# A cross-attention kernel with a small attention head section behind it: layer norms by a diagonal product, projections chunk by chunk, and the heads' exponents and copies dealt out anew

## What is computed

```python
def xattn(enc, dec):                       # enc = ctx (12544 rows), dec = layernorm(x) (128 rows)
    a = softmax(enc @ dec.T, axis=-1)      # over the 128 tokens
    return a.T @ enc
def attn(x):                               # 16 heads of 16 channels, causal
    q, k, v = split(x @ w_attn + b_attn)
    att = softmax(mask(q @ k.T / 4))
    return (att @ v) @ w_proj + b_proj
def ffn(x):
    return x @ W.T + b + (x @ V_r) @ C.T
x = x + xattn(ctx, layernorm(x))
x = x + attn(layernorm(x))
x = x + ffn(layernorm(x))
```

## Time and profile of the kernel before

| what | value |
|---|---|
| median of three executions | 108.64 us (108.2 to 108.72) |
| the profiled execution | 108.57 us |
| its span, first to last instruction | 106.6 us |
| TensorE, matmul busy | 102.2 us (96% of the span) |
| VectorE busy | 76.2 us (72%) |
| ScalarE busy | 72.7 us (68%) |
| GpSimd busy | 62.7 us (59%) |
| context and weights moved | 27.73 MB, no transfer in the last third but the result |

### The profile page before, as it was taken

How to read it: one execution, slowest core, us unless ns; L and a number is a source line. 1 busy time by engine, 2 the same in 40 slices (tenths; PEclk the granted TensorE clock), 3 DMA queues, 4 the chain that set the end, 5 groups by cost and what they waited for, 6 DMA issues and landing times.

```text
span 106.6 us, 2284 instructions
## 1 busy us (share of the span) xinstructions
PE 102.2 (96%) x756; PEld 88.2 (83%) x756; DVE 76.2 (72%) x217; ACT 72.7 (68%) x267; POOL 62.7 (59%) x45
## 2 busy tenths in 40 slices
PE   6999999999999999999999999999999999999990
PEld 1379999999999999999999999999998848756660
DVE  0413999968997777987777887777889765598331
ACT  4019999779997779777779777778879218297210
POOL 7405999949999767886767886767885020000020
PEclk9999999999999999999999999999999999999999
DMA  3999999999999999999999999950000000000001
GB/s 77 320 414 418 407 412 409 403 412 407 407 404 404 410 406 414 410 406 414 403 404 414 407 406 406 369 181 0 0 0 0 6 0 0 0 0 6 0 0 49
DMA packets 8604, 27.73 MB, mean 260 GB/s; under 512 B 1105, under 2 KB 1682, under 8 KB 8594
## 3 DMA queue, kind: packets, MB, share of 16 engines
q1 hardware_dynamic: 8594, 27.60, 66.2%
HBM read 27.46 MB, written 0.13 MB: 259 GB/s over the span
## 4 chain that ended last, share of the span: by engine, by line
PE 78%; issue 16%; DVE 2%; POOLq 1%; POOL 1%; DVEq 0%
PE bank L308 42%; PE bank L320 20%; PE bank L323 10%; PE bank L339 3%; PE bank L329 1%; PE bank L343 1%; PE bank L332 1%; PE bank L295 1%; POOLq L58 1%; POOL rstd L274 1%; DVE x L729 0%; DVE bn L581 0%; DVE x L659 0%; DVE mean_var L582 0%; DVE warm L597 0%
## 5 line engine op out<-in xcount | busy, mean ns | idle before, releaser
L282 POOL TENSOR_TENSOR rows_split<-rows_ring,rows_split 128x1024 fp32r<-128x1024 f32 (+1 forms) x25 | 58.4, 2336 | 18.3 <-ACT rows_split L490 18.3
L308 PE MATMUL bank<-query_t,cols_ring 128*128 128x128 f32 x392 | 47.7, 275 | 0.0
L308 PEld LDWEIGHTS bank<-query_t,cols_ring 128*128 128x128 f32 x392 | 45.8, 192 | 1.8 <-DVE query_t L595 0.6
L501 ACT ACTIVATE bank<-bank,neg_max 128x128 f32<-128x128 f32 x98 | 33.1, 337 | 11.1 <-DVE neg_max L619 10.9
L320 PE MATMUL bank<-rows_split,probs 128*128 128x512 f32 x92 | 34.8, 413 | 0.0
L490 ACT CAST rows_split<-rows_ring 128x1024 fp32r<-128x1024 f32 (+1 forms) x25 | 25.9, 1035 | 4.1 <-DMA rows_ring<-ctx_rows_dram 3.4
L636 DVE SCALAR_TENSOR_TENSOR probs<-bank,inv_sums,probs 128x128 fp32r<-128x128 f32 x98 | 27.6, 344 | 0.9
L323 PE MATMUL bank<-rows_split,probs 128*128 128x256 f32 x92 | 25.6, 279 | 0.0
L619 DVE TENSOR_REDUCE neg_max<-bank 128x4 f32<-128x512 f32 (+1 forms) x25 | 16.9, 675 | 12.0 <-PE bank L308 11.9
L320 PEld LDWEIGHTS bank<-rows_split,probs 128*128 128x128 f32 x92 | 17.4, 189 | 3.0
L501 ACT ACTIVATION_READ_ACCUMULATOR bank<-bank,neg_max 128x1 f32 x98 | 19.8, 202 | 0.0
(11 more groups left out here) (94 smaller groups left out, 66.1 us busy)
## 6 DMA issues: line engine op xcount, KB each, us to landing
cols_ring<-ctx_cols_dram SPq DMA_DIRECT2D x24, 512.0 KB, 14.7
rows_ring<-ctx_rows_dram SPq DMA_DIRECT2D x24, 512.0 KB, 15.2
wqk_sb<-w_qk_dram SPq DMA_DIRECT2D x1, 512.0 KB
cols_ring<-ctx_cols_dram SPq DMA_DIRECT2D x1, 256.0 KB, 10.8
rows_ring<-ctx_rows_dram SPq DMA_DIRECT2D x1, 256.0 KB, 10.3
wv_sb<-w_v_dram SPq DMA_DIRECT2D x1, 256.0 KB
wproj_sb<-w_proj_dram SPq DMA_DIRECT2D x1, 256.0 KB
wffn_sb<-w_ffn_dram SPq DMA_DIRECT2D x1, 256.0 KB
```

What stands on the lines that cost most here:

```text
L282: pool.tensor_tensor(rows_split[:, b, 0:n, 1, :], rows_ring[:, slot * STEP:slot * STEP + n, :], rows_split[:, b, 0:n, 0, :].bitcast(F32), ...
L308: last = pe.matmul(into[:, t * P:(t + 1) * P], cols_ring[:, slot * STEP + t, c, :], query_t[:, c, :], start=(c == 0), stop=(c == DC - 1))
L501: last = act.activation(on[:, t * P:(t + 1) * P], on[:, t * P:(t + 1) * P], ACT.Exp, bias=neg_max[:, b, t:t + 1], accum_out=sums[:, b, t:t ...
```

## The change

`layer_norm` no longer forms `normed`. VectorE subtracts the mean over all 256 channels into `centred`, before it waits for GpSimd, and then scales the identity with the inverse deviation into `rstd_diag`. `turn_normed` multiplies `centred` with that diagonal, a full fp32 product, where there was a transposition. The first score product and the first k product wait for the copy of the first half alone.

The projections run k chunk 0, q chunk 0, k chunk 1, q chunk 1, and each round of head scores waits for its own chunk. The bias of v comes as a 128-partition tile, added by VectorE, so the `ones` product goes.

In the heads, ScalarE takes all 16 exponents head by head; `shifted` and the reduction of `head_exp` go. VectorE copies all four groups out of PSUM. Banks, the order of the products on TensorE and that of VectorE's queue are new.

```diff
-        WARM_START, WARM_X, WARM_QUERY, WARM_EXPS, WARM_TURNS = 4, 3, 1, 5, (2, 3)
+        WARM_START, WARM_X, WARM_QUERY, WARM_EXPS, WARM_TURNS = 4, 3, 1, 5, (2, 2)
...
+                pe.wait_ge(centred_ready, n + 1)
+                pe.wait_ge(rstd_diag_ready, n + 1)
                 for c in range(DC):
-                    pe.wait_ge(normed_ready, DC * n + c + 1)
-                    pe.transpose(turn[c][:, 0:P], normed[:, c * P:(c + 1) * P], ident[:]).then_inc(turned, 1)
+                    pe.matmul(turn[c][:, 0:P], centred[:, c * P:(c + 1) * P], rstd_diag[:],
+                              start=True, stop=True).then_inc(turned, 1)
...
-            for n in [*range(DC, 2 * DC), *range(DC)]:
-                if n == DC + 1:
+            for n in [DC, 0, DC + 1, 1]:
+                if n == 1:
+
                     pe.wait_ge(wffn_ready, 1)
                 ps = q_ps[n][:, 0:P] if n < DC else k_ps[n - DC][:, 0:P]
                 for c in range(DC):
+                    if n == DC and c == 1:
+                        pe.wait_ge(turn_copied, 2)
...
-            pe.wait_ge(k_copied, 1)
-            pe.matmul(v_ps[:, 0:D], ones[:], bv_sb[:], start=True, stop=False, skip_group_check=True)
-            pe.wait_ge(k_copied, DC)
-            pe.wait_ge(q_copied, DC)
-
             for m in range(HM):
+
+                pe.wait_ge(k_copied, m // 2 + 1)
+                pe.wait_ge(q_copied, m // 2 + 1)
...
             turn_exps(1)
-            keep_warm(WARM_TURNS[1], exp_t_ps[2][:])
+            pe.matmul(x2_ps[:, 0:D], ident[:], x1_bias[:], start=True, stop=False, skip_group_check=True)
+            pe.wait_ge(x1_bias_centred_ready, 1)
+            pe.wait_ge(v_copied, 2)
+            for c in range(DC):
+                pe.matmul(x2_t_ps[c][:, 0:P], x1_bias_centred[:, c * P:(c + 1) * P], ident[:], start=True, stop=False,
+                          skip_group_check=True)
             turn_exps(2)
...
+            weigh_values(0)
+            keep_warm(WARM_TURNS[1], exp_t_ps[3][:])
             turn_exps(3)
             weigh_values(1)
+            spread_inverse(0)
+            weigh_values(2)
             spread_inverse(1)
...
-            exps_by_head(0)
-            exps_shifted(1)
-            exps_by_head(2)
-            exps_by_head(3)
-            copy_exp_t(2)
-            copy_exp_t(3)
+            for j in range(GROUPS):
+                exps_by_head(j)
...
+                dve.tensor_scalar(centred[:], src, mean_var[:, 0:1], None, ALU.subtract).then_inc(centred_ready, 1)
                 dve.wait_ge(rstd_ready, n + 1)
-                for c in range(DC):
-                    half = slice(c * P, (c + 1) * P)
-                    dve.tensor_scalar(normed[:, half], src[:, half], mean_var[:, 0:1], rstd[:, 0:1],
-                                      ALU.subtract, ALU.mult).then_inc(normed_ready, 1)
+                dve.tensor_scalar(rstd_diag[:], ident[:], rstd[:, 0:1], None, ALU.mult).then_inc(rstd_diag_ready, 1)
...
             for e in range(2):
-                dve.tensor_copy(v_pad[:, :, e, :, e * HD:(e + 1) * HD], v_view[:, :, e]).then_inc(v_copied, 1)
+                dve.tensor_tensor(v_pad[:, :, e, :, e * HD:(e + 1) * HD], v_view[:, :, e], bv_view[:, :, e],
+                                  ALU.add).then_inc(v_copied, 1)
+            copy_exp_t(0)
             dve.wait_ge(head_exp_ready, 2)
-            link(dve.tensor_reduce(head_sums[:, 0, 1, :], head_exp[:, 1], AX_X, ALU.add))
-            copy_exp_t(0)
             invert_sums(0)
             copy_exp_t(1)
+            copy_exp_t(2)
+            copy_inverse(0)
+            finish_y(0)
             dve.wait_ge(head_exp_ready, 4)
             invert_sums(1)
-            copy_inverse(0)
-            finish_y(0)
+            copy_exp_t(3)
             copy_inverse(1)
             finish_y(1)
```

More of the change, by code:

```diff
@@ L73, in perceiver_kernel @@
         x3 = sb("x3", [P, D])
-        normed = sb("normed", [P, D])
+        centred = sb("centred", [P, D])
+        rstd_diag = sb("rstd_diag", [P, P])
         normed_t = sb("normed_t", [P, DC, P])
@@ L92, in perceiver_kernel @@
         warm = sb("warm", [P, P], BF16)
-        ones = sb("ones", [1, P])
         in_head = sb("in_head", [P, P // HD])
@@ L110, in perceiver_kernel @@
         head_max = sb("head_max", [P, GROUPS, HM])
-        shifted = sb("shifted", [P, HM, P])
         head_exp = sb("head_exp", [P, GROUPS, HM, P])
@@ L134, in perceiver_kernel @@
         low_rank_ps = bank[7]
[L135 to L139 removed]
+        k_ps, q_ps, v_ps = [bank[2], bank[6]], [bank[5], bank[7]], bank[2]
+        exp_t_ps = [bank[5], bank[6], bank[7], bank[5]]
+        inv_ps = [bank[6], bank[7]]
+        y_t_ps = [bank[3], bank[4]]
+        x2_ps, x2_t_ps, ffn_ps = bank[0], [bank[1], bank[2]], bank[6]
         x_landed = sem("x_landed")
@@ L154, in perceiver_kernel @@
         rstd_ready = sem("rstd_ready")
-        normed_ready = sem("normed_ready")
+        centred_ready = sem("centred_ready")
+        rstd_diag_ready = sem("rstd_diag_ready")
         turned = sem("turned")
@@ L199, in perceiver_kernel @@
         out_stored = sem("out_stored")
-        weights = [(wqk_sb, w_qk), (bqk_sb, b_qk), (wv_sb, w_v), (bv_sb, b_v),
+        weights = [(wqk_sb, w_qk), (bqk_sb, b_qk), (wv_sb, w_v), (bv_sb, b_v.to_broadcast([P, D])),
                    (wproj_sb, w_proj), (bproj_sb, b_proj.to_broadcast([P, D])), (wffn_sb, w_ffn), (bffn_sb, b_ffn.to_broadcast([P, D])),
                    (vr_sb, v_r), (ct_sb, c_t)]
-        NCONSTS = 6
-        WARM_START, WARM_X, WARM_QUERY, WARM_EXPS, WARM_TURNS = 4, 3, 1, 5, (2, 3)
+        NCONSTS = 5
+        WARM_START, WARM_X, WARM_QUERY, WARM_EXPS, WARM_TURNS = 4, 3, 1, 5, (2, 2)
         block = ctx.enter_context(nc.Block())
@@ L254, in _ @@
             pool.memset(minus_half[:], -0.5).then_inc(consts_ready, 1)
-            pool.memset(ones[:], 1.0).then_inc(consts_ready, 1)
             pool.wait_ge(pool_step, 4)
@@ L307, in score @@
                     for c in range(DC):
+                        if s == 0 and t == 0 and c == 1:
+                            pe.wait_ge(turn_copied, 1)
                         last = pe.matmul(into[:, t * P:(t + 1) * P], cols_ring[:, slot * STEP + t, c, :],
@@ L548, in exps_by_head @@
                 last.then_inc(head_exp_ready, 1)
-            def exps_shifted(j):
-                act.wait_ge(shifted_ready, 1)
-                act.activation(head_exp[:, j], shifted[:], ACT.Exp).then_inc(head_exp_ready, 1)
-            def copy_exp_t(j):
-                act.wait_ge(exp_turned, j + 1)
-                act.copy(head_exp_t[:, j].rearrange("p m q -> p (m q)"), exp_t_ps[j][:])\
-                   .then_inc(exp_t_copied[j], 1)
-            exps_by_head(0)
-            exps_shifted(1)
-            exps_by_head(2)
-            exps_by_head(3)
-            copy_exp_t(2)
-            copy_exp_t(3)
+            for j in range(GROUPS):
+                exps_by_head(j)
             for c in range(DC):
@@ L601, in _ @@
             dve.wait_ge(eps_ready, 2)
+            dve.wait_ge(consts_ready, NCONSTS)
             dve.wait_ge(x_landed, 16)
@@ L700, in _ @@
             maximum_of_heads(1)
-            dve.wait_ge(head_max_ready, 2)
-            dve.tensor_tensor(shifted[:], by_head(head_scores[1]),
-                              head_max[:, 1, :].unsqueeze(2).to_broadcast([P, HM, P]),
-                              ALU.add).then_inc(shifted_ready, 1)
             maximum_of_heads(2)
```

25 lines of the change are left out of this document (4 added, 21 removed).

## The result

| what | before | after |
|---|---|---|
| median (20 executions each) | 108.50 us (108.07 to 109.04) | 108.90 us (108.61 to 109.53) |
| the profiled execution, its span | 108.57, 106.6 us | 108.83, 107.1 us |
| ratio after to before | | 1.0047, 95% interval 1.0033 to 1.0061 |

By the ratio the changed kernel is slower by 0.51 us (0.36 to 0.66); by the two medians it is 0.40. Both are under the 0.54 us that were set as the least that a measurement tells, but the interval is clear of 1.

A forecast was written before the change was run, and what follows sets the result against it. Bounds behind an unchanged stream: one line from norm to scores, then ScalarE, then TensorE. Terms 0 - 0.54 + 0.84 + 0.21 = +0.51 gave 109.15 us against a median of 108.64; range 108.7 to 109.9.

The forecast's parts named there:

- What bounds the kernel: Stream unchanged; behind it one line from second norm to head scores, then ScalarE to 97.34, then TensorE's back-to-back products.
- Start, 0: Start of the kernel: norm products cost 0.1 to 0.25 us, hidden; term 0, bounds 0 and +0.1.
- the cover by the fourth step's load: In the stream, TensorE waits 0.20 us at 11.82 for a transfer; a later start would shorten that wait.
- Norm to first maximum, -0.54: Second norm to first head maximum: -0.09 up to the first k product and -0.45 from the rounds.
- The rounds and chunks: Head scores: rounds 0 and 1 run in the wait for q chunk 1; -0.45 us, bounds 0 and -0.45.
- waiting for half: Second norm: k chunk 0 starts after ScalarE's copy, at 87.94 where it was 88.03 behind VectorE's copy.
- rival C: `centred` beside GpSimd's power delays it at the second norm: +0.4 us, 109.55; chance 0.13.
- Exponents, +0.84: Heads on ScalarE: group 1 by heads takes 1.38 us where at once took 0.54, without gaps; +0.84.
- VectorE's queue, +0.21: Last exponent to group 3's values: group 3's copy queues behind inverse copy 0; 3.21 us for 3.00, bounds -0.1 and +0.4.
- The end, 0: Behind group 3's values: the same TensorE products, not y, end last; term 0.
- Rival A: Behind the last exponent, TensorE's own order decides: 2.15 us instead of 3.00, -0.55 in all, 108.1; chance 0.08.
- Rival B: TensorE's clock falls to 1.2 GHz behind 101 us after a queue gap: about +2, 111; chance 0.07.

The follow-up runs named there:

- E7: E1 with TensorE taking group 1's values and the first spread ahead of group 3's transposition, replacing two products of zeros; 107.53 us, ratio to before 0.9912.
- E12: Changed kernel with group 3's copy first on VectorE and group 1's exponents at once, diagonal norm kept, a repeat run; 107.18 us, ratio to before 0.9875.
- E5: Changed kernel with the norm and transposition of before, the rest kept; 108.62 us, ratio to before 1.0008.
- E2: Changed kernel with group 1's exponents as before: `shifted`, taken at once, summed by VectorE; 108.38 us, ratio to before 0.9974.
- E1: Changed kernel with the inverse of the second sums and group 3's copy ahead of inverse copy 0 and y half 0's finish on VectorE; 108.02 us, ratio 0.9934.
- E8: The kernel of E12 without the two products of zeros ahead of group 3's transposition; 107.41 us, ratio to before 0.9884.
- E10: The kernel of E12 with the norm and transposition of before and without the two products of zeros; 106.84 us, ratio to before 0.9844.
- E11: The kernel of E12 with the norm of before and E7's TensorE order, no zeros; 107.35 us, ratio to before 0.9904.
- E4: Changed kernel with `centred` behind VectorE's wait for GpSimd, so it doesn't overlap the power; 109.42 us, ratio to before 1.0069.

## Why the prediction came out right

- *What bounds the kernel.* Right: stream unmoved, then one line, then ScalarE, then TensorE, which waits for VectorE's queue.
- *Start, 0.* Near: +0.1 us by ratio, pieces and the time outside the span, not clear of 0. In the seven profiles whose start is that of the changed kernel the second norm starts at 85.12 in the mean (84.86 to 85.39), in the five with the old norm and the first-half wait at 85.08 (84.95 to 85.25), so no cost of the diagonal shows there. The reason given, the cover by the fourth step's load, isn't borne out: that load shows no wait in the changed kernel, where there was 0.20, but 0.54 in E7 and 0.24 in E12 with the same start. Later starts are partly made up all the same: the first score product starts between 5.76 and 6.82, and 78.8 to 79.4 us pass from there to the second norm, the fewest behind the latest starts.
- *Outside the span.* The forecast carried the 2 us around the span over unchanged. It is 0.23 less, and no term of the sum stands for it.
- *Norm to first maximum, -0.54.* Measured -0.44. The rounds and chunks gave -0.41 behind the first k product (91.20 less 87.85, against 91.79 less 88.03), predicted -0.45. The step that failed is the one before it, norm to first k product, put at -0.09 and measured -0.03. Its parts by E5: waiting for half -0.22, as in the forecast's own chain; the diagonal +0.19, forecast +0.13. In that: power +0.17 (put at 0 in the sum, priced in rival C), the wait that is no longer an instruction of its own -0.08 (not foreseen), the diagonal itself -0.05 (-0.06), product +0.15 (+0.19).
- *Exponents, +0.84.* Measured +0.87, and E2 takes exactly that back.
- *VectorE's queue, +0.21.* Measured +0.23, each link of the forecast's chain within 0.02 of its row, and E1 shows the mechanism: nothing but the place of the copy, and of the inverse of the second sums, in the queue.
- *The end, 0.* Measured 0, and 0 in all variants but E7, E8, E10 and E11, where TensorE reaches the projection before the first half of y is finished.
- *Rival A* is ruled out for the change by the gap of 0.79 at 100.24. Its arithmetic was right: E1 is rival A (2.19 for 2.15).
- *Rival B* didn't occur: the granted clock reads 1.00 in every stretch, and for the profiled executions of E8 and E10, without the zeros, too. Whether transpositions are left out of what the clock counts, as the Trainium skill ("TensorE: Matmul & The Clock Gate", Part 4: PE-mode transpose) has it, no run here shows.
- *Rival C* was real in kind and smaller in size: +0.17 at the second norm, not +0.4, and 0.08 of it given back. One of the forecast's own signs of being wrong was a power longer than 0.6 us; it took 0.73, so by that sign the account of this step failed, though the total didn't. The traces fit a GpSimd that goes on for its first 0.14 us and is then held until `centred` is done. The overlap, from the start of the power to the end of `centred`, is 0.23 at the start and 0.30 at the second norm, the power is longer by 0.09 and 0.17, and the difference is 0.14 and 0.13. All seven profiles with that overlap agree within 0.01. An even slowing would take the same share of both, but 0.09 is 0.4 of 0.23, and 0.17 is 0.55 of 0.30. Two lengths of overlap don't prove it. The Trainium skill ("GPSIMD Engine Reference", 1. Specifications) has the two engines contend for their shared SBUF interfaces, where VectorE's instruction runs in a two-port mode or has two inputs in SBUF. The trace agrees in that the power takes 0.73 beside `centred` and 0.56 without; no row shows in which mode `centred` runs. A chance of 0.13 was too low for the mechanism and about right for its full price.

The sum of the forecast was +0.51, and so is the ratio's difference, but not for the same reasons. The pieces gave +0.65: the norm to the first maximum was 0.10 worse than forecast, the exponents and the queue 0.05 worse in sum. Against that stand the 0.23 us outside the span, which the forecast had no term for. That the total fits to a hundredth is luck; that it fits within 0.3 is not, since every term of the 21 us was read from a row and came within 0.1. The first maximum, too, came at 91.20 for the forecast's 91.25 only because the second norm started 0.15 earlier in this execution.

## What to carry to other kernels

An edit that moves work to an engine with idle time must be read in that engine's queue: the idle 1.5 us of VectorE was a wait, with the copy that everybody needed standing behind it. Take a change of several parts apart before judging it: here one part was worth -0.66 us and the three others (the diagonal, the exponents, VectorE's queue) together +1.3 in the traces, and the total looked like nothing. And after each gain ask anew which engine ends last, since an order (E7, E11) or a filler (the zeros in E2 and E8, by the traces) that is free or good under one limit costs under the next. Last, compare times and spans side by side: when they differ by another amount than before, a part of the change lies where no row shows it.

## What the runs showed of the hardware

- An operation of GpSimd on one element per partition (the power) took 0.55 to 0.57 us alone, 0.64 with `centred` beside it at the start and 0.72 to 0.73 at the second norm. In the other direction, `rstd_diag` took 0.52 us beside GpSimd's memset of `v_pad` at the start, and 0.29 alone. In the kernel before, the two halves of `normed` took 0.60 together with that memset beside them and 0.60 without, so not every operation of VectorE is held up.
- VectorE started 0.03 us behind GpSimd's end when its operation waits itself, and 0.11 behind it when a wait of its own stands between the two (before, E4, E5).
- From the start of an fp32 product of 128 columns on TensorE to the start of ScalarE's copy of its result it is 0.49 us (87.04 to 87.53), from the start of a transposition 0.34.
- ScalarE's exponents with sum start every 0.34 us throughout, but each is recorded as longer, from 0.37 (91.92) to 0.45 (97.07): in this row of instructions the stride counts, not the duration.
- At the start, the pair of norm products took from 0.68 to 1.20 us (E4), and the pair of transpositions 0.49 or 0.69, in profiles whose granted clock reads 1.00 there. What makes the difference isn't shown by any row.
